# All keys and values made in the first layer, the last feed-forward's hidden tiles turned as fp32 by quarters, and a store moved behind a row's load

## What is computed

```python
x = x + tanh(g_xattn[0]) * ssm(ctx, layernorm(x), L0...)      # 16 states, scan along 512 rows
x = x + tanh(g_ffn[0])   * gated_top2_ffn(layernorm(x))       # 2:4 sparse hidden, 2048 wide
x = x + tanh(g_xattn[1]) * one_head_attention(layernorm(x), ctx)
x = x + tanh(g_ffn[1])   * ternary_ffn(layernorm(x))          # 1408 wide
x = x + tanh(g_xattn[2]) * ssm(ctx, layernorm(x), L2...)
x = x + tanh(g_ffn[2])   * fp8_ffn(layernorm(x))              # 1536 wide
x = x + tanh(g_xattn[3]) * attention16(layernorm(x), ctx)     # below
x = x + tanh(g_ffn[3])   * bit_ffn(layernorm(x))              # below
```

```python
h = bitlinear(x, w1, b1)             # activation rows rounded to 8 bits, weights to -1, 0, 1
h = layernorm(gelu(h), gamma, beta)  # 2048 wide
return bitlinear(h, w2, b2)          # h scaled per row, rounded to whole numbers up to 127
```

## Time and profile before

| | |
|---|---|
| time, median of 3 runs | 3708.42 us (3700.74 to 3710.17) |
| profiled execution | 3708.7 us, its span 3707.1 us |
| busy share of the span | PE 93%, DVE 81%, ACT 47%, POOL 17% |
| chain that ended last | PE 48%, DVE 27%, issue 14%, ACT 6%, DMA 3% |
| mean granted TensorE clock | 0.966 |
| instructions | 40267 |

### The profile page before, as it was taken

How to read it: one execution, slowest core, us unless ns; L and a number is a source line. 1 busy time by engine, 2 the same in 40 slices (tenths; PEclk the granted TensorE clock), 3 DMA queues, 4 the chain that set the end, 5 groups by cost and what they waited for, 6 DMA issues and landing times.

```text
span 3707.1 us, 40267 instructions
## 1 busy us (share of the span) xinstructions
PE 3437.8 (93%) x12305; PEld 1947.9 (53%) x12322; DVE 3013.5 (81%) x4951; ACT 1759.9 (47%) x2748; POOL 623.9 (17%) x596
## 2 busy tenths in 40 slices
PE   7888888799999999899999899999999999999887
PEld 4667676544444444444445788655455455455443
DVE  8899998797979798789889867688388388388797
ACT  6878787633333223334443311255155155155297
POOL 2324251243433220134331000000000000000000
PEclk9899988999999999999999999999999999999998
DMA  4324241524342322443444300221021022021000
GB/s 156 133 65 148 66 147 59 196 86 147 102 153 93 137 84 92 156 153 97 149 156 175 145 24 23 104 70 60 31 70 60 21 70 70 20 70 64 32 12 34
DMA packets 91260, 345.73 MB, mean 93 GB/s; under 512 B 11841, under 2 KB 20161, under 8 KB 77793
## 3 DMA queue, kind: packets, MB, share of 16 engines
q1 hardware_dynamic: 61552, 226.90, 17.4%
q0 software_dynamic: 29552, 116.94, 9.6%
HBM read 280.88 MB, written 62.91 MB: 93 GB/s over the span
## 4 chain that ended last, share of the span: by engine, by line
PE 48%; DVE 27%; issue 14%; ACT 6%; DMA 3%; DVEq 0%; POOL 0%; ACTq 0%; POOLq 0%; SPq 0%
PE ps L1213 30%; PE ps L1610 6%; PE ps L1600 3%; DVE room L1782 3%; PE ps L1441 2%; DVE room L1786 2%; DMA room<-bc_scratch 2%; DVE room L1790 2%; PE ps L1493 2%; PE ps L1282 2%; DVE room L1852 1%; DVE room L1795 1%; DVE room L1850 1%; ACT room L871 1%; DVE room L2320 1%
## 5 line engine op out<-in xcount | busy, mean ns | idle before, releaser
L1213 PE MATMUL ps<-lnT,room 128*128 128x512 f32 x2240 | 987.0, 596 | 23.1 <-DVE room L2007 16.0
L1213 PEld LDWEIGHTS ps<-lnT,room 128*128 128x128 f32 x2240 | 426.0, 191 | 567.9 <-issue 525.5
L1213 PE MATMUL ps<-room 128*128 128x512 f32 (+2 forms) x1807 | 666.8, 524 | 49.6 <-ACT room L1138 21.1
L680 POOL TENSOR_TENSOR idle<-idle 128x1 f32<-128x1 f32 x268 | 447.1, 1668 | 1263.4 <-ACT room L881 434.6
L1213 PEld LDWEIGHTS ps<-room 128*128 128x128 f32 (+1 forms) x1824 | 289.9, 163 | 404.5 <-issue 258.4
L1441 PE MATMUL ps<-room 128*128 128x512 f32 x864 | 379.7, 597 | 8.5 <-DVE room L1961 8.5
L792 ACT ACTIVATE room<-room,small 128x511 f32<-128x511 f32 x256 | 163.6, 710 | 380.6 <-DVE room L1786 380.5
L1852 DVE TENSOR_TENSOR_SCAN room<-room 128x2048 f32<-128x2048 f32 x64 | 283.2, 4425 | 19.0 <-ACT room L871 13.8
L1786 DVE TENSOR_TENSOR_SCAN room<-room 128x2048 f32<-128x2048 f32 x64 | 283.4, 4428 | 5.9 <-DVE room L1782 0.9
L1441 PEld LDWEIGHTS ps<-room 128*128 128x128 f32 x864 | 165.1, 192 | 215.2 <-issue 208.3
L1112 ACT ACTIVATE room<-ps,stat 128x512 f32<-128x512 f32 x256 | 199.0, 777 | 137.3 <-DVE stat L2268 137.3
(11 more groups left out here) (284 smaller groups left out, 5105.1 us busy)
## 6 DMA issues: line engine op xcount, KB each, us to landing
room<-in_ffn SPq DMA_DIRECT2D x16, 2048.0 KB, 10.9
room<-bc_scratch POOLq DMA_DIRECT2D x128, 256.0 KB, 3.6
room<-kv_stash SPq DMA_DIRECT2D x64, 512.0 KB, 3.4
kv_stash<-room POOLq DMA_DIRECT2D x96, 256.0 KB, 2.4
room<-stash POOLq DMA_DIRECT2D x24, 1024.0 KB, 5.2
room<-in_ffn SPq DMA_DIRECT2D x20, 1024.0 KB, 5.1
room<-in_ffn SPq DMA_DIRECT2D x24, 768.0 KB, 5.6
room<-in_ffn SPq DMA_DIRECT2D x12, 1536.0 KB, 7.3
```

Of the source, the lines that this page charges most:

```text
L680: nc.gpsimd.tensor_tensor(idle[:, :], idle[:, :], idle[:, :], ALU.add).then_inc(zeros_added, 1)
L1213: last = nc.tensor.matmul(out, lhsT, rhs, start=(i == 0), stop=(i == len(parts) - 1))
```

## The change

Keys and values: `KV_HEADS` = 12 becomes `H` = 16, so the first layer makes all of them, 16 units per batch. `KV_ORDER` puts unit 0 at state 1 (was 4), units 7 and 8 at state 9 and 9 and 10 at state 10, then one at each state from 11 to 15. The context for the next batch is loaded at n == 15. `gate_mamba` loses its units with their loads, copies, stores, weights, semaphores and the waits on them in later stages; ScalarE widens the weights in groups of four, two and two.

SyncE: the store of Du moves from n == 8 to n == 9, behind the load of row 9 (and behind the small store at that state).

Last feed-forward: `quantize` keeps only its first pass, which leaves whole numbers plus the rounding constant in fp32. TensorE turns these fp32 tiles in four quarters of four, alternating between banks 5 and 6, and ScalarE takes each quarter with the constant subtracted into bf16, right behind `quantize`. TensorE does `out(u)` ahead of `hidden(u + 3)`. VectorE does `final(u - 2)` first in its step.

```diff
-KV_HEADS, KV_LEAD = 12, 4
-KV_OWN = KV_HEADS - KV_LEAD
-KV_ORDER = (4, 5, 6, 6, 7, 8, 8, 9, 10, 11, 12, 13)
+H, KV_LEAD = 16, 4
+KV_OWN = H - KV_LEAD
+KV_ORDER = (1, 5, 6, 6, 7, 8, 8, 9, 9, 10, 10, 11, 12, 13, 14, 15)
...
-                        if n == 10 and not last:
+                        if n == 15 and not last:
                             sp.wait_ge(tile_filled, tile("kv", KV_OWN - 1, 1)[0] + 1)
                             sp.dma_start(m_kctx, ctx_d[bass.ds(b * P + P, P), :]).then_inc(kctx_loaded, 16)
...
-                        if n == 8:
+                        if n == 9:
                             place = stashed(2, b)
                             sp.wait_ge(Du_ready, b + 1)
                             sp.dma_start(place, m_z).then_inc(Du_stored, 16)
...
             def gate_mamba(stage):
-                sp.wait_ge(a_qk, 2 * B)
-                sp.dma_start(ctx[:, :], ctx_d[0:P, :]).then_inc(gk_loaded[0], 16)
                 sp.wait_ge(s_y_added, 2 * B * STATES)
-                for i in range(LATE):
-                    h = KV_HEADS + i
-                    sp.dma_start(g_kvw[:, i * HEAD_KV:(i + 1) * HEAD_KV], head_d[h * P:(h + 1) * P, HEAD_Q:]
-                                 ).then_inc(gkw_loaded, 16)
...
-                units(0, 1)
                 gate(0)
-                units(1, 2)
                 gate(1)
-                units(2, 5)
                 gate(2)
-                widen(0, 2)
-                units(5, 9)
-                widen(2, 4)
+                widen(0, 4)
                 gate(3)
                 widen(4, 6)
-                units(9, 13)
                 take_lnT(stage + 1, 0)
                 widen(6, EARLY)
-                units(13, B * LATE)
...
                 def take_hqT(u):
-                    act.wait_ge(b_htr, u + 1)
+
                     act.wait_ge(b_mm2, u)
-                    nc.scalar.activation(b_hqT, psb(5, 2), ACT.Copy).then_inc(b_hT_ready, 1)
+                    for q in range(4):
+                        act.wait_ge(b_htr, 4 * u + q + 1)
+                        nc.scalar.activation(b_hqT[:, q * 512:(q + 1) * 512], ps[:, 5 + q % 2, :], ACT.Identity, bias=unrnd
+                                             ).then_inc(b_hT_ready, 1)
...
                     nc.scalar.activation(b_ga[j % 2], b_ga[j % 2], ACT.Identity, scale=sc2[:, j % 2:j % 2 + 1], bias=rnd
-                                         ).then_inc(b_round, 1)
-                    act.wait_ge(b_round, u + 1)
-                    act.wait_ge(b_htr, u)
-                    nc.scalar.activation(b_hq, b_ga[j % 2], ACT.Identity, bias=unrnd).then_inc(b_hq_ready, 1)
+                                         ).then_inc(b_hq_ready, 1)
...
                     quantize(u, j)
+                    take_hqT(u)
                     if u + 2 < B * NT:
-                        act.wait_ge(b_hq_ready, u + 1)
                         gelu(u + 2)
...
                         deviations(u + 2)
-                    take_hqT(u)
...
                 gate(0)
-                units(3, 6)
                 gate(1)
-                units(6, 10)
                 gate(2)
-                units(10, 13)
-                pe.wait_ge(gk_taken, 26)
                 transpose_ln(stage + 1, 0)
                 gate(3)
                 pe.wait_ge(lnT_ready, B * LNT[stage + 1] + 1)
-                units(13, B * LATE)
...
                     pe.wait_ge(b_hq_ready, u + 1)
-                    for f in range(NF):
-                        mm = nc.tensor.transpose(psb(5, 2)[:, f * P:(f + 1) * P], b_hq[:, f * P:(f + 1) * P], identb_)
-                    mm.then_inc(b_htr, 1)
+                    for q in range(4):
+
+                        if 4 * u + q >= 2:
+                            pe.wait_ge(b_hT_ready, 4 * u + q - 1)
+                        for f in range(4):
+                            mm = nc.tensor.transpose(ps[:, 5 + q % 2, f * P:(f + 1) * P],
+                                                     b_ga[u % 2][:, (4 * q + f) * P:(4 * q + f + 1) * P], ident[:, :])
+                        mm.then_inc(b_htr, 1)
...
                     turn_hidden(u)
+                    out(u)
                     if u + 3 < B * NT:
                         hidden(u + 3)
-                    out(u)
...
+                    if u >= 2:
+                        final(u - 2)
                     dve.wait_ge(b_sq, u + 1)
...
-                    if u >= 2:
-                        final(u - 2)
                     mx = stat[:, 78:79]
```

More of the change, by code:

```diff
@@ L278, in flamingo @@
         b_w1, b_w2 = b_w[:, 0:NK * F3], b_w[:, NK * F3:]
[L279 removed]
+        b_xqT, b_hqT, b_dev = (v.bitcast(BF16) for v in (b_xqT, b_hqT, b_dev))
         def psb(bank, n=1):
@@ L631, in attention3 @@
                 for parity in range(2):
-                    sp.wait_ge(kv_stored[parity], B * KV_HEADS * 16)
-                for i in range(3):
-                    sp.wait_ge(gk_stored[i], GK_STORES[i] * 16)
+                    sp.wait_ge(kv_stored[parity], B * H * 16)
                 for h in range(2):
@@ L702, in store_kv @@
                                b * KV_WAITS + (KV_FIRST + 2 * i),
[L703 to L709 removed]
+                               None if last and i + 2 >= slots else (h + 2) % H, i)
             def feed_states(stage, s):
@@ L980, in gate @@
                     nc.scalar.activation(g_z[b % 2], ln[:, :], ACT.Silu).then_inc(g_z_ready, 1)
-                def units(first, last):
-                    for k in range(first, last):
-                        if k >= 3:
-                            act.wait_ge(gk_stored[k % 3], k // 3 * 16)
-                        for half in range(2):
-                            act.wait_ge(gk_filled, 2 * k + half + 1)
-                            nc.scalar.activation(g_kv[k % 3][:, half * 4 * HD:(half + 1) * 4 * HD],
-                                                 ps[:, 4 + 2 * (k % 2) + half, :], ACT.Copy).then_inc(gk_taken, 1)
                 def widen(first, last):
@@ L2066, in body @@
                             t = g * n + j
-                            if first and t == n:
-                                for i in range(3):
-                                    dve.wait_ge(gk_stored[i], GK_STORES[i] * 16)
                             dve.wait_ge(up_done, b * T + (base + t + 1))
```

68 lines of the change are left out of this document (14 added, 54 removed).

## The result

The changed kernel takes 3761.3 us (median of four runs, 3759.2 to 3765.7) against 3709.3 us for the kernel before; the ratio is 1.0137, with a 95% interval of 1.0115 to 1.0158. That is slower by 43 to 59 us. The forecast was 3741 us, with 3757 us as its upper end: the direction was right, the size was not. The profiled execution after has a span of 3758.6 us, 51.5 more than the one before.

What follows compares the result with a forecast made beforehand. VectorE was taken to bound the first layer and last feed-forward, TensorE the gating stage. First layer +35, gating stage -6.3, last feed-forward +4 sum to +32.7 us, giving 3741 us; range 3699 to 3757.

Steps and rivals of the forecast that it cites:

- the price of the units' stores in the first layer: First layer, behind state 10: unit 10's take waits for unit 9's store, until 356.0; store waits at unit 12 about 0.5.
- TensorE's turns in the gating stage: Gating stage: turns 1.9 us in each 12.9; 9.5 us saved, 3.2 lost to the next stage's slow start, net -6.3.
- the walk: First layer, full batch state by state: softplus +5.2 us, state 13's scan +7.6, about +10 in all, bounds +6 and +13.
- the first rival: First layer: units wait for TensorE only, stores in time; +6.5 us per full batch, +0.5 last, 3721 us; chance 0.20.
- The last batch: First layer: no exponential at state 9, but units 7 to 11 and z's silu precede decay 13; +5 us, bounds +0.5, +8.
- The unit at state 1: First layer: unit 0 at state 1 delays decay 5 by 2.5 us, ending in the wait for the exponential.
- Rival 2: First layer: added units fit, TensorE filling each before ScalarE arrives; full batches 0, last -4.6 us, 3693 us; chance 0.16.
- Rival 3: First layer: stash stores collide, landings 8 us instead of 2.4; +13 per batch, +8 last, 3755 us; chance 0.12.

Runs made afterwards that it cites:

- everything mended: Changed kernel with units in spread order, no one-column operation, exponential ahead of unit 8, stash store behind row 9, old last feed-forward: 3695.9 us; mended twelve units: 3684.8.

## Why the prediction was right in direction and wrong in size

The measured time lies 4 us above the range's upper end and 20 above the forecast. The step that failed is the price of the units' stores in the first layer; a second, smaller one is that of TensorE's turns in the gating stage.

**Direction and place: right.** The first layer lost, the gating stage gained a little, the last feed-forward lost 3.4 us where 4 was said, with steps of 11.46 us to the hundredth. VectorE waits for w2's product in them. The wait of 4.69 us went, that for the exponential grew to 8.42 (about 9 was said), state 13's scan waits for its decay, y's product for TensorE.

**The term that was mis-sized: the stores of the units.** The prediction had GpSimd's small operation, with its 3.96 us, at one place: unit 10. For units 11 to 15 it added "about 0.5" for store waits, and its rival without store waits stood 15 us below it in the first layer (20 against 35). Without the operation the first layer's batches are shorter by 8.2, 9.7, 7.1 and 14.2 us, 39 us in all. But the kernel before gains by its removal too, 17 us there, so the two kernels have to be set side by side with the operation in both or in neither. In both, the change costs 57 us in the first layer. In neither, its batches of 168.5, 166.0, 166.4 and 149.4 us become 175.3, 177.6, 177.6 and 154.2: +6.8, +11.6, +11.2 and +4.8, together 34 us, where 10, 10, 10 and 5 were said. So the forecast is about what the change costs when no store is held up, and the 22 us that it missed come of the change and the operation together (with the stash store behind row 9 in the kernel before as well, the change costs 66 us with the operation and 38 without). In whole times the change costs 34 us without the operation (3690.3 to 3724.4) and 52 with it. That they meet so closely is partly luck, for the walk had the operation in it once and no price for units at the lower clock.

Against the kernel before as it is, the kernel without the operation has +3.5, +6.9, +7.0 and +0.2. These are close to the first rival's numbers (+6.5 and +0.5), but not its mechanism, "units wait for TensorE only": ScalarE still waits 28.7 us for stores, half the products gained 10 us, and other places of the units 23.

The mechanism was in the text; it was priced at one unit of a batch and not at each store behind state 10. The row in which it stood is the earlier trace rows: 14.3 us of one batch, 41.8 of the layer, of which 0.7 is left in the run without the operation. The prediction read the wait at 347.09 as a slow landing, and rightly: the operation ahead of that store took 0.20 us. Three of the layer's 21 waits, of 2.0 to 2.2 us, are of this kind, with landings of 8.2 or 8.3. Of the others all but one of 0.4 us follow a store whose operation took 0.6 to 4.2 us.

The Trainium skill (SBUF — State Buffer, "Who interferes with whom") gave the rule: a VectorE operation with two SBUF inputs holds up a GpSimd operation that reads SBUF, not one that only writes it. The traces agree with the first half: 3.80 us for one column under a scan. Issuing a DMA took 0.54 us under one, and whether that is a case of the second half no run here shows. The error was in counting how often the rule would act.

**The last batch: +5 forecast, +14.4 measured.** The prediction carried over the walk of the full batches. In fact VectorE waits there for the turned tiles of states 10 and 11, 5.79 and 7.35 us, behind ScalarE's waits for stores of 5.59, 5.11 and 6.86:

```profile
726.48 2.29 DVE L1781 TENSOR_TENSOR room<-room 128x2048 f32<-128x2048 f32 x1 [5.79 <-PE ps L1233]
...
742.35 2.29 DVE L1781 TENSOR_TENSOR room<-room 128x2048 f32<-128x2048 f32 x1 [7.35 <-PE ps L1233]
```

Without the operation in either kernel this batch goes from 149.4 to 154.2 us, the forecast's +5. The other 10 us hung on the operation.

**The unit at state 1: later than said.** The prediction had 2.5 us of delay from it, ending in a wait of VectorE that was there anyway. State 5 was late by 4.9 us, and that took back the vanished wait for row 9. It did end in the wait for the exponential, as said, which is 8.42 us long in this batch. Whether it cost the batch anything is not shown, since no run moves this unit alone.

**TensorE's clock behind its new gaps.** The prediction charged 3.62 us for each unit. Two of the second batch's units ran mostly at the lower clock (0.58 granted), in 6.37 and 6.29 us (at 397.13). The first of them:

```profile
376.48 6.37 PE L1164 MATMUL ps<-down_rows,room 128*128 128x256 f32 x16 [2.33 <-ACT room L826]
```

That is 2.7 us more each, both behind state 10, where TensorE is on the path. Most of it hangs on the operation as well: without it the first of them takes 5.44 and the second 3.72.

**The gating stage: -2.2 instead of -6.3.** The step that failed is "TensorE then only turns tiles, 1.9 us in each 12.9". It idles 10.24 us between its turns, and 16 of them then take 3.67 or 3.68 us at a granted clock of 0.50, the lower of its two levels:

```profile
2096.34 3.68 PE L1316 MATMUL ps<-ident,room 128*128 128x128 f32 x16 [10.24 <-DVE room L1868]
...
2121.97 3.68 PE L1158 MATMUL ps<-ident,ln 128*128 128x128 f32 x16 [8.04 <-DVE ln L1687]
2125.44 2.23 PE L1316 MATMUL ps<-ident,room 128*128 128x128 f32 x16
```

VectorE takes the tiles as they come, so that its cycle grew from 12.9 to 13.9 us, and in its last one the turn of the next stage's input stands ahead as well (a wait of 2.29). VectorE's own chain, up to the cut of the next stage's input, is 68.8 us long instead of 69.1 (2065.50 to 2134.25, against 2012.06 to 2081.14): what TensorE's units had cost it, the slow turns took back. The 4.5 us between the cut and the first product did go. The prediction set the rule of the Trainium skill (TensorE: Matmul & The Clock Gate, "Part 4: PE-mode transpose"), that turning doesn't release the full clock, against the start of the next stage alone, 3.2 us (2.5 measured: 19.14 us for its first 72 products instead of 16.63). The slow turns of this stage itself had no price.

The traces don't agree with that rule as it was used. In the last two rows above 32 turns follow each other behind 8.04 us of idleness, with no product among them: the granted clock is 0.50 over the first 16, 0.62 up to 2126.30 and 1.00 from there on, so it was at its full level while the engine only turned. The same 32 turns stand in all twelve kernels with the emptied stage; the second 16 take from 1.91 to 3.07 us, against 3.32 to 3.47 from the first 16's start to theirs. Each slow set of this stage stands behind 8 to 20 us of idleness, and the next stage's first products, too, start behind 6.68 us of it. The prediction's "No row here shows a stretch of turns alone" was a misreading: the earlier trace rows has 32 of them in 6.59 us, with a granted clock of 0.50 up to 396.50 and 0.60 behind it.

**Rival 2** (the units fit) is out: no batch grew by less than 11 us. **Rival 3**, the collision of the stash store with the others, named the right symptom and 3755 us, but another cause; the changed kernel's stores landed in a median of 2.6 us (before 2.4), and 30 of 128 took over 4 us to land (before 20 of 96). With the stash store in its old place the full batches were no shorter (188.6 to 191.9 us). In the last batch, though, the three waits above end with landings of 4.2 to 4.7 us; what of them is landing and what is issue was not separated.

**What stays open.** With everything mended, four units in the first layer still cost 11 us more than in the gating stage; the traces put it into the full batches (VectorE waits 2.57 us for y's product in the second) without one wait that makes up the sum. And why half the products gain only 10 us, with the operation or without, is not settled beyond the clock's fall (to 0.84 in the second batch with it). The two profiled executions without the operation lie 18.7 us apart, 17 of them in the first layer, where the medians lie 10 apart, so the spread among executions is nearly as large as what is to be explained.

## What to carry to other kernels

A small operation ahead of a store is not free because it is small: look at its longest, not its mean (4.2 and 1.3 us in the changed kernel's first layer), and at who waits for what stands behind it. Before you say what such an operation costs a change, take it out of both kernels. Ask of each wait for a DMA whether it is the transfer, or the issue that came late; here the two had the same releaser in the view of waits. And when work is moved out of a stage that TensorE fills, what is left there can run at the lower clock: here 16 turns took 3.7 us behind 10 us of idleness instead of 1.9. Price the remaining turns at that length, each time they occur.

## What the runs showed of the hardware

The one-column operation of GpSimd took 0.19 us beside an idle VectorE and up to 4.3 us beside a scan, ending with it. Issuing a DMA from the same engine took 0.54 us inside a scan. Taking the operation out gave 22 us in the kernel before and 37 in the changed one. TensorE's granted clock reached 1.00 in a stretch of turns alone (2126.30 to 2127.70 in the trace of after).

Stages that the change doesn't touch were 6.5 us shorter in the profiled execution. In the first feed-forward two steps of 1.7 us each can be followed, and the first is this: 32 products behind a gap of TensorE that is as long as before. Before, and then after:

```profile
885.86 15.70 PE L1441 MATMUL ps<-room 128*128 128x512 f32 x32 [2.09 <-DVE room L1961]
```

```profile
942.62 14.00 PE L1368 MATMUL ps<-room 128*128 128x512 f32 x32 [2.06 <-DVE room L1892]
```

After the same 2.1 us of idleness, with the same turns and products ahead at the full clock, the same 32 products took 15.70 us in one execution and 14.00 in the other; the granted clock was 0.89 and 1.00. So a gap of this length may or may not be paid for, and a part of the spread of 10 us and more among the runs of one kernel may come from there; that was not tested.
